# The last product in three fp32r passes instead of two column halves, and one expert tile moved ahead of the second token turn

## The chip, the cores and the metric

The kernel runs on one core of one Trainium2 chip. The metric is the device time of one execution in microseconds (us). The engines that matter are TensorE (PE in the profile: matrix products and transposes), VectorE (DVE), ScalarE (ACT), GpSimd (POOL) and SyncE (SP, whose queue issues the loads). They run side by side and wait for each other on semaphores.

## What is computed

A perceiver block over B = 2 batches of 128 tokens of width 512, with 2048 context rows for each batch, 16 heads, and a feed-forward layer with 4 experts of width 2048. All data is float32. Cut to what matters:

```python
x = x + cross_attention(layernorm(x), ctx, ctx)            # 16 heads, 2048 keys
x = x + self_attention_block(layernorm(x))                 # 16 heads, own residual and layernorm

def ffn(x):                                                # x: (256, 512), called on layernorm(x)
    expert_idx = argmax(x @ W_router)                      # 4 experts
    h = gelu(einsum('th,ehi->tei', x, W1) + b1)            # W1: (4, 512, 2048)
    intermediate = einsum('te,tei->ti', onehot(expert_idx), h)
    y = intermediate @ Wo + bo + x                         # Wo: (2048, 512)
    return layernorm(y) * gamma + beta
x = x + ffn(layernorm(x))
```

## The kernel before

All engines run programs written out by hand, in the order of the code; there is no scheduler. Where one engine needs another's result it waits for a semaphore's count, and everything behind that wait on its engine stands too.

**Two ways to multiply.** A product of float32 operands can be given to TensorE as it is ("whole"). Or each operand is split: a rounded high part H (type fp32r) and the rest L = x - H, and three products HH, HL and LH are added up in PSUM ("three passes"). The large products of the kernel are of the second kind. ACT, POOL or DVE makes H by a copy with a cast, DVE makes L by a subtraction.

**Stages.** The keys, values, scores and the softmax of the cross-attention for batch 0 and then batch 1 take up to about 360 us, eight head groups p after each other, four context chunks c in each (`keys`, `values`, `scores`, `probs_T`, `weighted_values`). In the first group, p = 0, the values V of a chunk are made by four products j = 0 to 3 between `keys(0, c)` and `scores(0, c)`. ACT copies V for j = 0 and 2, DVE for j = 1 and 3. The self-attention of batch 0 lies inside the batch-1 work.

**The expert layer.** W1 comes as 16 tiles of 128 x 2048, first for batch 0 (`first_experts(n)`, tile FIRST[n]) and then again for batch 1 (`second_experts(n)`, tile n). Since the tokens of batch 0 are ready first, PE runs batch 0's tiles between the steps of batch 1's self-attention. Tiles 0, 1, 2, 3 and 14 (WHOLE) are multiplied whole, line 1409, the rest in three passes, lines 1419 to 1421. The H of a tile is line 631 on ACT (line 404 on POOL), its L is line 979 on DVE (`first_low`).

**The token turn.** After tile 12 (n = 12) PE does `normalized_T(1)` (four transposes of the normalized tokens, line 1141, which wait for DVE's `normalize`, line 710), `expert_bias(0)` (line 1446), `logits(1)` (line 1147 with 4 output columns), then tile 13, `masks(1)` and `onehots_T(1)` (lines 1393 and 1401), tile 14 and tile 15. DVE meanwhile does `first_low(13)`, `logits(1)` (line 908), `router(1)`, the token's low part, `first_low(15)`, `onehots_T(1)`, the masked tokens (`masked_both(0)`, line 931) and then the L part of each tile of the second round, line 1121.

**The second round.** `second_experts(n)` are lines 1460 to 1462: 12 passes of 512 columns for each tile. ACT makes w2H (line 644) when a buffer of three is free, DVE makes w2L (line 1121). Between these tiles PE transposes batch 0's hidden units (`hidden_T(0, c)`) and multiplies them by Wo, four quarters of the 2048 hidden units, `ffn_out(0, c)`, line 1478, 4 whole products each.

**The end.** After the last tile PE does `ffn_out(0, 3)`, then `hidden_T(1, c)` for c = 0 to 3 (line 1141), then batch 1's product with Wo in two column halves, line 1604: 16 whole products of 256 columns for columns 0 to 255, and 16 for the others. ACT (line 557) and DVE (line 944) copy the transposed hidden units to SBUF in turn. `finish(b)` on DVE adds the residual, computes mean and variance, and scales. In batch 1 it takes each half as it comes, lines 955 and 956. One step in it is POOL's power for the inverse root, line 378.

## Time and profile before

| | |
|---|---|
| time, median of 3 runs | 516.69 us (516.57 to 518.53) |
| the profiled execution's own time | 517.64 us |
| its span in the trace | 515.9 us |
| granted TensorE clock, mean | 0.995 |
| PE busy | 498.3 us, 97% of the span |
| DVE busy | 299.4 us, 58% |
| ACT busy | 259.8 us, 50% |
| chain that ended last | PE 79%, ACT 9%, DVE 7%, issue 4%, POOL 1% |

Read the table as the frame: the span is what the trace covers, and 1.7 us of the profiled execution's time lie outside it. PE is busy nearly all the time, and 79% of the chain that ended last is PE's own work, so what counts is which instructions PE has to run and where it stands still. A matmul's row shows its latency, not the time that it keeps the engine; the time between the starts of two matmuls is the rate.

### The profile page before, as it was taken

The page shows a single profiled execution, that of the slowest core. Times are in us where ns is not written, and L with a number is a line of the kernel's source. Part 1 is how long each engine was busy: PE and PEld are TensorE (multiplying, and loading weights), DVE is VectorE, ACT ScalarE, POOL GpSimd, SP SyncE. Part 2 cuts the span into 40 slices and gives each one's busy share as a digit, 9 for nine tenths or more (in the row PEclk, how much of TensorE's full clock was granted, in tenths as well). Part 3 has the DMA queues.
Part 4 walks back from the last instruction along what each step waited for, and adds up shares of the span by engine and source line. Part 5 has one row for each costly group of instructions (what it writes and reads, how often), then busy time and mean ns, then how long its engine had stood idle before and what let it go on. Part 6 is the DMA issues. An engine that isn't in the chain of part 4 may idle for free.

```text
span 515.9 us, 9281 instructions
## 1 busy us (share of the span) xinstructions
PE 498.3 (97%) x3762; PEld 383.1 (74%) x3762; DVE 299.4 (58%) x583; ACT 259.8 (50%) x396; POOL 42.2 (8%) x34
## 2 busy tenths in 40 slices
PE   8999999999999999999999999999999999999995
PEld 6886776777777777887877778757695777877664
DVE  4647523546455542436286474588479988965532
ACT  4130119494858641238267649476255735754310
POOL 0220000000298000000000000000002010000000
PEclk9999999999999999999999999999999989999999
DMA  8800000000440022220300000495586998874000
GB/s 290 344 0 1 1 1 0 3 0 3 151 168 11 1 83 83 81 83 1 142 3 2 0 3 1 147 422 249 180 327 248 361 402 302 334 292 164 1 20 20
DMA packets 11497, 63.52 MB, mean 123 GB/s; under 512 B 1600, under 2 KB 2112, under 8 KB 4544
## 3 DMA queue, kind: packets, MB, share of 16 engines
q1 hardware_dynamic: 11168, 62.67, 32.1%
q8 instruction: 30, 0.49, 0.4%
q10 hardware_dynamic: 288, 0.27, 0.2%
q14 instruction: 11, 0.09, 0.1%
HBM read 62.41 MB, written 0.52 MB: 122 GB/s over the span
## 4 chain that ended last, share of the span: by engine, by line
PE 79%; ACT 9%; DVE 7%; issue 4%; POOL 1%; POOLq 0%; ACTq 0%; DVEq 0%
PE ps L1147 35%; PE ps L1217 11%; PE ps L1231 6%; PE ps L1201 5%; ACT Pm L447 4%; PE ps L1460 3%; PE ps L1462 3%; PE ps L1461 3%; PE ps L1478 3%; PE ps L1604 2%; PE ps L1409 1%; ACT PT L455 1%; PE ps L1141 1%; PE ps L1243 1%; DVE w1L L979 1%
## 5 line engine op out<-in xcount | busy, mean ns | idle before, releaser
L455 ACT COPY PT<-ps 128x512 f32<-128x512 f32 x128 | 68.5, 592 | 28.9 <-PE ps L1217 28.9
L745 DVE TENSOR_SCALAR_CACHE_REDUCE Pm<-ps,small 128x512 f32<-128x512 f32 x96 | 66.4, 748 | 28.5 <-PE ps L1201 28.4
L1217 PE MATMUL ps<-ident,Pm 128*128 128x128 f32 x512 | 69.3, 277 | 2.9 <-ACT Pm L447 2.9
L1217 PEld LDWEIGHTS ps<-ident,Pm 128*128 128x128 f32 x512 | 56.5, 141 | 17.7 <-issue 11.0
L447 ACT ACTIVATE Pm<-Pm,small 128x2048 f32<-128x2048 f32 x32 | 64.3, 2011 | 7.4 <-DVE Pm L745 7.3
L725 DVE SCALAR_TENSOR_TENSOR KrL<-ps,small,KrH 128x512 fp32r<-128x512 f32 x32 | 23.9, 747 | 59.2 <-ACT KrH L433 59.2
L1147 PE MATMUL ps<-ctxH,wkH 128*128 128x512 f32 x124 | 51.3, 414 | 0.0
L1147 PE MATMUL ps<-wvH,ctxH 128*128 128x512 f32 x124 | 50.1, 404 | 1.0 <-DVE V L734 1.0
L1147 PE MATMUL ps<-ctxL,wkH 128*128 128x512 f32 x124 | 48.6, 392 | 0.0
L1147 PE MATMUL ps<-ctxH,wkL 128*128 128x512 f32 x124 | 48.5, 391 | 0.0
L1147 PE MATMUL ps<-wvH,ctxL 128*128 128x512 f32 x124 | 48.4, 390 | 0.0
L1147 PE MATMUL ps<-wvL,ctxH 128*128 128x512 f32 x124 | 48.3, 390 | 0.0
L433 ACT ACTIVATE KrH<-ps,small 128x512 fp32r<-128x512 f32 x32 | 22.0, 688 | 44.4 <-PE ps L1147 43.7
L1121 DVE TENSOR_TENSOR w2L<-w2raw,w2H 128x2048 fp32r<-128x2048 f32 x16 | 36.4, 2289 | 11.8 <-ACT w2H L644 11.8
L644 ACT CAST w2H<-w2raw 128x2048 fp32r<-128x2048 f32 x16 | 30.6, 1911 | 19.0 <-PE ps L1462 15.0
L1231 PE MATMUL ps<-PT,V 128*32 128x128 f32 x1024 | 34.6, 276 | 1.0 <-ACT PT L455 1.0
L378 POOL TENSOR_TENSOR small<-small 128x1 f32<-128x1 f32 x10 | 6.8, 678 | 332.3 <-DVE small L706 332.3
L442 ACT COPY V<-ps 128x512 f32<-128x512 f32 x16 | 9.4, 585 | 46.6 <-PE ps L1147 43.9
L1231 PEld LDWEIGHTS ps<-PT,V 128*32 128x32 f32 x1024 | 26.0, 109 | 8.2 <-issue 6.0
L1147 PEld LDWEIGHTS ps<-ctxH,wkH 128*128 128x128 f32 x124 | 23.5, 190 | 10.0 <-issue 5.7
L734 DVE COPY V<-ps 128x512 f32<-128x512 f32 x16 | 11.0, 689 | 33.1 <-PE ps L1147 33.0
L1147 PEld LDWEIGHTS ps<-wvH,ctxH 128*128 128x128 f32 x124 | 23.3, 188 | 7.4 <-DVE V L734 1.4
(219 smaller groups left out, 859.8 us busy)
## 6 DMA issues: line engine op xcount, KB each, us to landing
w1raw<-in_W SPq DMA_DIRECT2D x16, 1024.0 KB, 6.1
w2raw<-in_W SPq DMA_DIRECT2D x16, 1024.0 KB, 5.5
raw<-in_ctxT SPq DMA_DIRECT2D x7, 1024.0 KB, 5.0
woF<-in_ffn_Wo SPq DMA_DIRECT2D x4, 1024.0 KB, 9.2
wo<-in_wo SPq DMA_DIRECT2D x2, 1024.0 KB, 4.8
ctx_first<-in_ctxT SPq DMA_DIRECT2D x4, 256.0 KB, 5.0
wv_raw<-in_xWv SPq DMA_DIRECT2D x2, 512.0 KB, 7.4
wq<-in_xWq SPq DMA_DIRECT2D x1, 1024.0 KB, 12.2
```

The source lines that it names most:

```text
L433: act.activation(KrH[:, c % KR, :], ps[:, bank, :], ACT.Identity, bias=bias3[:, 1, p % G:p % G + 1], scale=1.0).then_inc(k_hi, 1)
L447: act.activation(Pm[:, i, :], Pm[:, i, :], ACT.Exp, bias=mx[:, p % 2, i, C - 1:C], scale=-1.0, accum_out=den[:, p, i:i + 1]).then_inc(exp_ ...
L455: act.copy(PT[:, c % 2, i, :, :].rearrange("p k t -> p (k t)"), ps[:, t_bank(p, c, i), :]).then_inc(pt_done, 1)
L644: act.copy(w2H[n % 3][:], w2raw[n % RING2][:]).then_inc(w1_hi, 1)
L725: dve.scalar_tensor_tensor(KrL[:, c % KR, :], ps[:, bank, :], bias3[:, 1, p % G:p % G + 1], KrH[:, c % KR, :].bitcast(F32), ALU.add, ALU.s ...
L745: dve.tensor_scalar(Pm[:, i, c * CH:(c + 1) * CH], ps[:, i, :], -1.0, mx[:, p % 2, i, c - 1:c] if c else NOT_YET, ALU.mult, ALU.min, accum ...
L1121: dve.tensor_tensor(w2L[n % RING2][:], w2raw[n % RING2][:], w2H[n % 3][:].bitcast(F32), ALU.subtract).then_inc(w1_split, 1)
L1147: mm = pe.matmul(dst, l, r, start=(n == 0), stop=(n == len(pairs) - 1))
L1201: last = pe.matmul(ps[:, i, :], l[q, g, b * T:(b + 1) * T], r[q, c % KR, :], start=(k == 0), stop=(k == len(terms) - 1))
L1217: last = pe.transpose(ps[:, t_bank(p, c, i), j * P:(j + 1) * P], Pm[:, i, c * CH + j * P:c * CH + (j + 1) * P], ident[:])
L1231: last = pe.matmul(ps[q, PV_BANK, 0:T], V[:, c * JT + j, (HPG * g + i) * DH:(HPG * g + i + 1) * DH], PT[:, c % 2, i, j, :], start=(c == 0 ...
L1460: pe.matmul(dst, zH[:, n, :], wH[:, cc], start=(n == 0), stop=False)
```

## The change

Two larger edits and two small ones.

1. **Batch 1's product with Wo.** The column halves are gone. The hidden units of quarter 3 are multiplied whole (4 products of 512 columns), those of quarters 0 to 2 (12 products) in three passes each. For this ACT makes woH (three casts of 128 x 2048, line 691 of the new kernel) after its last w2H and before batch 1's gelu, and DVE makes woL in place of woF (three subtractions, line 1132) after its last w2L. PE transposes quarter 3 first. ACT copies all four quarters (line 696), three of them as the high part hidTH, and DVE makes hidTL (line 1138) before `finish(0)`. `finish(1)` is now the same as `finish(0)`, on all 512 columns after the last pass. `ffn_out` raises f_mm after every quarter, so that DVE knows when it may overwrite woF.
2. **Tile 14 ahead of the turn.** FIRST has 14 before 13, and three tiles (11, 12, 14) instead of two stand between `attention2_out(1)` and the turn. Its load is issued before `second_in(1)` instead of behind it.
3. **Scores of the last chunk in group 0.** `scores(0, 3)` stands behind the first V product of chunk 3 and not behind the fourth. DVE reads those scores before it copies V for j = 1 and 3.
4. Some pairs of semaphores (one for each batch) become one semaphore that counts on; the waits are for the same events.

```diff
-        FIRST = (0, 1, 4, 5, 6, 2, 3, 7, 8, 9, 10, 11, 12, 13, 14, 15)
+        FIRST = (0, 1, 4, 5, 6, 2, 3, 7, 8, 9, 10, 11, 12, 14, 13, 15)
...
             first_in_(13)
-            second_in(1)
             sp.wait_ge(first_tile, USED[9])
             first_in_(14)
+            second_in(1)
...
+            act.wait_ge(woF_in, 16 * KT)
+            for c in range(SPLIT_WO):
+                act.wait_ge(w1_tile, 11 + c)
+                act.copy(woH[c][:], woF[:, KT * c:KT * (c + 1), :]).then_inc(wo_hi, 1)
             gelu(1, range(IC))
-            hidden_T(1, 0)
-            hidden_T(1, 2)
+            for k, c in enumerate((3, 0, 1, 2)):
+                act.wait_ge(hT_mm[1], k + 1)
+                dst = hidTW if c == 3 else hidTH[:, KT * c:KT * (c + 1), :]
+                act.copy(dst[:].rearrange("p k t -> p (k t)") if c == 3 else dst.rearrange("p k t -> p (k t)"),
+                         ps[:, 4 + c, :]).then_inc(hT_act[1], 1)
...
+            for c in range(SPLIT_WO):
+                k = slice(KT * c, KT * (c + 1))
+                dve.wait_ge(wo_hi, c + 1)
+                dve.wait_ge(f_mm, c + 1)
+                dve.tensor_tensor(woL[:, k, :], woF[:, k, :], woH[c][:].bitcast(F32), ALU.subtract).then_inc(wo_split, 1)
             ffn_residual(0)
             ffn_residual(1)
+            for c in range(SPLIT_WO):
+                k = slice(KT * c, KT * (c + 1))
+                dve.wait_ge(hT_act[1], c + 2)
+                dve.tensor_tensor(hidTL[:, k, :], split4(ps[:, 4 + c, :]), hidTH[:, k, :].bitcast(F32), ALU.subtract)\
+                   .then_inc(hT_dve[1], 1)
             finish(0)
-            hidden_T(1, 1)
-            hidden_T(1, 3)
             finish(1)
...
                 for j in range(JT):
                     values(0, c, j)
-                scores(0, c)
+                    if c == C - 1 and j == 0:
+                        scores(0, c)
+                if c < C - 1:
+                    scores(0, c)
...
-            for c in range(KT):
+            for c in (3, 0, 1, 2):
                 hidden_T(1, c)
-            for h in range(2):
-                cols_h = slice(h * CH // 2, (h + 1) * CH // 2)
-                for k in range(IT):
-                    if h == 0 and k % KT == 0:
-                        c = k // KT
-                        pe.wait_ge(hT_dve[1] if c % 2 else hT_act[1], c // 2 + 1)
-                    last = pe.matmul(ps[:, 1 + h, 0:CH // 2], hidT[1][:, k, :], woF[:, k, cols_h], start=(k == 0),
-                                     stop=(k == IT - 1))
-                last.then_inc(f_mm, 1)
+            pe.wait_ge(hT_act[1], 1)
+            pe.wait_ge(hT_dve[0], 1)
+            for k in range(KT):
+                pe.matmul(ps[:, 1, :], hidTW[:, k, :], woF[:, 3 * KT + k, :], start=(k == 0), stop=False)
+            for c in range(SPLIT_WO):
+                pe.wait_ge(wo_split, c + 1)
+                pe.wait_ge(hT_dve[1], c + 1)
+                for k in range(KT):
+                    hH, hL = hidTH[:, KT * c + k, :], hidTL[:, KT * c + k, :]
+                    pe.matmul(ps[:, 1, :], hH, woH[c][:, k, :], start=False, stop=False)
+                    pe.matmul(ps[:, 1, :], hH, woL[:, KT * c + k, :], start=False, stop=False)
+                    last = pe.matmul(ps[:, 1, :], hL, woH[c][:, k, :], start=False,
+                                     stop=(c == SPLIT_WO - 1 and k == KT - 1))
+            last.then_inc(f_mm, 1)
```

How this changes the order in which instructions stand on an engine is shown at the two places that matter.

PE around the token turn, before: `w1H_D` is tile 12, `attnT` the tokens that are turned, `small,qT` the logits, `w1H_A` tile 13, `w1raw_136` tile 14, `w1H_B` tile 15.

```order
L1421 MATMUL ps<-w1H_D,z0L 128x512
L1141 MATMUL ps<-ident,attnT 128x128 x4
L1446 MATMUL ps<-b1H,ohT_121 128x512 x4
L1446 MATMUL ps<-b1L,ohT_121 128x512 x4
L1147 MATMUL ps<-small,qT 128x4 x4
L1419 MATMUL ps<-w1H_A,z0H 128x512
...
L1393 MATMUL ps<-ident,oh_124 128x128 x4
L1401 MATMUL ps<-ident,oh_124 128x128
L1409 MATMUL ps<-w1raw_136,z_129 128x512 x4
L1419 MATMUL ps<-w1H_B,z0H 128x512
```

The same place in the changed kernel, whose lines are numbered anew.

```order
L1432 MATMUL ps<-w1H_D,z0L 128x512
L1420 MATMUL ps<-w1raw_136,z_129 128x512 x4
L1149 MATMUL ps<-ident,attnT 128x128 x4
L1457 MATMUL ps<-b1H,ohT_121 128x512 x4
L1457 MATMUL ps<-b1L,ohT_121 128x512 x4
L1155 MATMUL ps<-small,qT 128x4 x4
L1430 MATMUL ps<-w1H_A,z0H 128x512
...
L1404 MATMUL ps<-ident,oh_124 128x128 x4
L1412 MATMUL ps<-ident,oh_124 128x128
L1430 MATMUL ps<-w1H_B,z0H 128x512
```

Tile 14 went from behind the one-hot transposes to ahead of the token transposes, and tile 15 now follows the one-hot transposes directly.

DVE from the last tile of the second round to the end, before.

```order
L1121 TENSOR_TENSOR w2L_160<-w2raw_154,w2H_163 128x2048
L938 TENSOR_TENSOR attnT<-attnT,rowsF 128x4x128
...
L939 TENSOR_TENSOR x_sb<-x_sb,rowsF 128x512
L961 TENSOR_TENSOR u_119<-ps,attnT 128x512
...
L965 SCALAR_TENSOR_TENSOR u_119<-u_119,small,x_sb 128x512
L944 COPY hidT_172<-ps 128x512 x2
L955 TENSOR_TENSOR uo_173<-ps,attnT 128x256
L956 BN_STATS small<-uo_173 128x6
L955 TENSOR_TENSOR uo_173<-ps,attnT 128x256
L956 BN_STATS small<-uo_173 128x6
```

And in the changed kernel.

```order
L1121 TENSOR_TENSOR w2L_160<-w2raw_154,w2H_163 128x2048
L1132 TENSOR_TENSOR woL<-woF,woH_174 128x2048
L1132 TENSOR_TENSOR woL<-woF,woH_175 128x2048
L1132 TENSOR_TENSOR woL<-woF,woH_176 128x2048
L948 TENSOR_TENSOR attnT<-attnT,rowsF 128x4x128
...
L949 TENSOR_TENSOR x_sb<-x_sb,rowsF 128x512
L1138 TENSOR_TENSOR hidTL<-ps,hidTH 128x512 x3
L961 TENSOR_TENSOR u_119<-ps,attnT 128x512
...
L961 TENSOR_TENSOR uo_173<-ps,attnT 128x512
L712 BN_STATS small<-uo_173 128x6
```

Six subtractions are new on DVE: three large ones ahead of the residuals and three small ones ahead of `finish(0)`, where two copies had stood behind it. The half-width additions and statistics became full-width ones.

## Rows read from the trace of the kernel before

**Rows 1.** Timeline, PE at the end: start us, us, engine, line, operation, [idle before].
```profile
489.63 3.59 PE L1478 MATMUL ps<-woF,hidT 128*128 128x512 f32 x8
...
493.06 1.91 PE L1141 MATMUL ps<-ident,hid 128*128 128x128 f32 x16
...
494.80 1.89 PE L1604 MATMUL ps<-woF,hidT 128*128 128x256 f32 x8
...
497.73 12.35 PE L1604 MATMUL ps<-woF,hidT 128*128 128x256 f32 x56 [1.03 <-DVE hidT L944]
```
**Rows 2.** The same timeline, first and last pass of one second-round tile's stretch.
```profile
486.90 0.39 PE L1460 MATMUL ps<-w2H,zH 128*128 128x512 f32 x1
...
489.40 0.39 PE L1462 MATMUL ps<-w2H,zL 128*128 128x512 f32 x1
```
**Rows 3.** The same timeline, DVE: `finish(0)`'s first and last step, then `finish(1)`'s.
```profile
493.33 0.69 DVE L961 TENSOR_TENSOR u<-ps,attnT 128x512 f32<-128x512 f32 x1 [8.95 <-PE ps L1478]
...
496.32 0.75 DVE L965 SCALAR_TENSOR_TENSOR u<-u,small,x_sb 128x512 f32<-128x512 f32 x1 [0.51 <-POOL small L378]
...
510.19 0.42 DVE L955 TENSOR_TENSOR uo<-ps,attnT 128x256 f32<-128x256 f32 x1 [6.09 <-PE ps L1604]
...
512.68 0.75 DVE L965 SCALAR_TENSOR_TENSOR uo<-uo,small,x_sb 128x512 f32<-128x512 f32 x1 [0.51 <-POOL small L378]
```
**Rows 4.** The same timeline, ACT and DVE ahead of the end.
```profile
477.37 1.90 ACT L644 CAST w2H<-w2raw 128x2048 fp32r<-128x2048 f32 x1 [0.80 <-PE ps L1462]
...
479.30 2.29 DVE L1121 TENSOR_TENSOR w2L<-w2raw,w2H 128x2048 fp32r<-128x2048 f32 x1 [0.41 <-ACT w2H L644]
...
487.78 2.64 ACT L552 ACTIVATE hid<-ps 128x512 f32<-128x512 f32 x4 [8.51 <-PE ps L1462]
...
493.69 0.59 ACT L557 COPY hidT<-ps 128x512 f32<-128x512 f32 x1 [3.27 <-PE ps L1141]
```
**Rows 5.** Timeline, PE around the token turn.
```profile
418.32 0.39 PE L1421 MATMUL ps<-w1H_D,z0L 128*128 128x512 f32 x1
419.59 0.66 PE L1141 MATMUL ps<-ident,attnT 128*128 128x128 f32 x4 [0.87 <-DVE attnT L710]
...
421.01 1.10 PE L1147 MATMUL ps<-small,qT 128*128 128x4 f32 x8
421.97 0.78 PE L1419 MATMUL ps<-w1H_A,z0H 128*128 128x512 f32 x1
...
426.33 0.60 PE L1393 MATMUL ps<-ident,oh 128*128 128x128 f32 x4
...
433.08 0.39 PE L1460 MATMUL ps<-w2H,zH 128*128 128x512 f32 x1
```
**Rows 6.** Stretches: us, busy of PE, PEld, DVE, ACT, POOL, then granted clock, DMA.
```profile
422.00:425.00 3.00, 3.00 (x8) 2.42 (x9) 2.62 (x8) 2.95 (x2) 0.00 (x0) 0.50 0.99 418
```
**Rows 7.** Timeline, DVE behind the turn.
```profile
422.14 0.16 DVE L908 COPY small<-ps 128x4 f32<-128x4 f32 x1 [0.41 <-PE ps L1147]
...
424.00 2.28 DVE L979 TENSOR_TENSOR w1L<-w1raw,w1H_B 128x2048 fp32r<-128x2048 f32 x1
427.08 0.29 DVE L927 CAST ohT<-ps 128x128 fp32r<-128x128 f32 x1 [0.80 <-PE ps L1401]
...
428.80 4.49 DVE L1121 TENSOR_TENSOR w2L<-w2raw,w2H 128x2048 fp32r<-128x2048 f32 x2
```
**Rows 8.** Timeline, SyncE's queue: the load of tile 14.
```profile
407.14 0.33 SPq L298 DMA_DIRECT2D w1raw<-in_W  x1
```
**Rows 9.** The page's DMA issues: KB each, median us from issue to landing.
```profile
w1raw<-in_W SPq DMA_DIRECT2D x16, 1024.0 KB, 6.1
```
**Rows 10.** Timeline, PE and ACT between group 0 and group 1.
```profile
76.87 2.01 ACT L447 ACTIVATE Pm<-Pm,small 128x2048 f32<-128x2048 f32 x1 [3.82 <-DVE Pm L745]
...
78.62 0.39 PE L1147 MATMUL ps<-ctxL,wkH 128*128 128x512 f32 x1
...
79.05 0.69 ACT L433 ACTIVATE KrH<-ps,small 128x512 fp32r<-128x512 f32 x1
```

More of the change, by code:

```diff
@@ L152, in perceiver_block @@
         uo = [u[0], at("uo_1", [P, D], F32, 182)]
+        SPLIT_WO = 3
+        woH = [at(f"woH{c}", [P, KT, D], F32R, kb) for c, kb in enumerate((64, 80, 128))]
+        woL = at("woL", [P, SPLIT_WO * KT, D], F32R, 96)
+        hidTH = at("hidTH", [P, SPLIT_WO * KT, T], F32R, 56)
+        hidTW = at("hidTW", [P, KT, T], F32, 62)
+        hidTL = at("hidTL", [P, SPLIT_WO * KT, T], F32R, 184)
         col = [0]
@@ L247, in perceiver_block @@
             sem("v2T_mm"), sem("v2_ready"), sem("pv2_mm"), sem("rden_ready"), sem("cN_ready"))
-        cT_dve, cT_act, o2_mm, u_done = each("cT_dve"), each("cT_act"), sem("o2_mm"), sem("u_done")
+        cT_dve, cT_act, o2_mm, u_done = sem("cT_dve"), sem("cT_act"), sem("o2_mm"), sem("u_done")
         x2T_mm, x2T_done, logit_mm, logit_done, z_ready = (
@@ L504, in features @@
                     act.activation(dst[b][:, m, :], ps[:, QKV_BANKS[b][k], m * T:(m + 1) * T], ACT.Identity,
-                                   bias=b2[:, k, m:m + 1], scale=1.0).then_inc(ready[b], 1)
-                act.wait_ge(ready[b], KT)
+                                   bias=b2[:, k, m:m + 1], scale=1.0).then_inc(ready, 1)
+                act.wait_ge(ready, KT * (b + 1))
             def exponentials2(b, i):
@@ L800, in _ @@
                     split(c + 1)
-                for j in (1, 3):
-                    values(0, c, j)
+                if c < C - 1:
+                    values(0, c, 1)
+                    values(0, c, 3)
                 if c == 1:
@@ L1475, in ffn_out @@
                 pe.wait_ge(woF_in, 16 * KT)
+                if c == 0 and b:
+                    pe.wait_ge(hT_dve[0], 1)
                 pe.wait_ge(hT_dve[b] if c % 2 else hT_act[b], c // 2 + 1)
@@ L1575, in _ @@
             attention2_out(1)
-            for n in range(11, 13):
+            for n in range(11, 14):
                 first_experts(n)
@@ L1595, in _ @@
             ffn_out(0, 3)
-            for c in range(KT):
+            for c in (3, 0, 1, 2):
                 hidden_T(1, c)
-            for h in range(2):
-                cols_h = slice(h * CH // 2, (h + 1) * CH // 2)
-                for k in range(IT):
-                    if h == 0 and k % KT == 0:
-                        c = k // KT
-                        pe.wait_ge(hT_dve[1] if c % 2 else hT_act[1], c // 2 + 1)
-                    last = pe.matmul(ps[:, 1 + h, 0:CH // 2], hidT[1][:, k, :], woF[:, k, cols_h], start=(k == 0),
-                                     stop=(k == IT - 1))
-                last.then_inc(f_mm, 1)
+            pe.wait_ge(hT_act[1], 1)
+            pe.wait_ge(hT_dve[0], 1)
+            for k in range(KT):
[9 more added lines that the diff above has]
+                                     stop=(c == SPLIT_WO - 1 and k == KT - 1))
+            last.then_inc(f_mm, 1)
 ROWS = ("L0_xattn_bo", "L0_attn_bo", "L0_attn_beta", "L0_attn_gamma",
```

54 lines of the change are left out of this document (21 added, 33 removed).

## The prediction

> **What bounds the kernel now.** I read the page first: PE is busy for 97% of the span and carries 79% of the chain that ended last, so only PE's instructions and its halts count. Then the timeline of the last 26 us, since most of the diff is there. PE never stops from the last expert tile to the transposes; then come 8 half-width matmuls, a halt for DVE's copy of the hidden units, and 56 more [rows 1]. Behind PE's last matmul there is only `finish(1)`, on DVE and POOL [rows 3]. Then the token turn: PE halts for 0.87 us for the normalized tokens, does small work up to 421.97 [rows 5], and the granted clock of the next three microseconds is 0.50, that is 1.2 GHz instead of 2.4 [rows 6]. Last the border of groups 0 and 1 [rows 10].
>
> **The rates.** A whole product of 512 columns is two matmul records; four take from 489.63 to 493.06, 3.43 us, or 0.857 each [rows 1]. A half-width matmul takes 12.35 / 56 = 0.2205 us, so a half product takes 0.441 and the 32 of them 64 x 0.2205 = 14.1 us [rows 1]. An fp32r pass of 512 columns takes (489.40 - 486.90) / 11 = 0.2273 us [rows 2], so three passes take 0.682, less than the whole product's 0.857.
>
> The Trainium skill ("TensorE: Matmul & The Clock Gate", Back-to-back issue gap) gives columns / 2.4 GHz plus 2.5 ns for a lone matmul's gap, 216 ns here. The measured 227 ns is what I use; by the page's figure the new end would be 0.4 us shorter still, by an estimate.
>
> **Edit 1, the end.** Both kernels reach the first product with Wo at about 494.7: `ffn_out(0, 3)` ends at 493.06 and the 16 transposes take 1.64 us [rows 1]. Before, from there to PE's end at 510.08: 14.1 us of matmuls and a gap of 497.73 - 494.70 - 8 x 0.2205 = 1.27 us behind the DVE copy [rows 1]; 15.4 together. Now: 4 whole products, 3.43, and 36 passes, 36 x 0.2273 = 8.18; 11.6 together, if nothing waits. PE is done at 506.3, 3.8 us earlier.
>
> Does anything wait? Each new operand in turn. woH: ACT's last w2H ends at 479.27 [rows 4]. The buffers that woH overwrites belong to tiles 10, 11 and 12, which are done by then (the last cast itself waited for tile 12), so three casts of 1.90 end at 485.0. Gelu begins at 487.78 [rows 4]: 2.8 us of slack, and the casts cost nothing. woL: DVE is free at 481.6, three subtractions of 2.29 end at 488.5 [rows 4], and the two residual pairs, four full-width steps of 0.69 [rows 3] and their waits, 2.9 us, at 491.4. hidT: the first transposes are quarter 3's, which needs the last gelu. That ends at 487.78 + 2.64 = 490.4, covered until 493.06 by `ffn_out(0, 3)`. ACT's copy starts at 493.69 and lasts 0.59 [rows 4], so it ends at 494.28, before 494.7. Then three more copies, about 0.5 us apart, end near 495.8, and DVE's three hidTL of about 0.69 near 496.8. The first pass needs the first of them at 494.7 + 3.43 = 498.1. So this wait has 2.5 us of slack. The DVE halt vanishes, and no other takes its place. `finish(0)` is moved behind hidTL and runs from about 496.8 to 500.6; its store is long over at the end.
>
> The end behind PE gets longer. `finish(1)` was half-width, from 510.19 to 513.43, 3.24 us. Now it is full-width, as `finish(0)` is: 493.33 to 497.07, 3.74 us [rows 3]. So 0.5 us are lost there, and I allow 0.1 for the wider last matmul. Sum of edit 1: 3.8 - 0.5 - 0.1 = **3.2 us** gained. Bounds: 2.2 us (one more halt of about 1.0, like the one of rows 1) and 3.6.
>
> **Edit 2, tile 14 ahead.** It is multiplied whole, 3.43 us, from 418.55 to 421.98. Its load is issued at 407.14 and no longer behind that of a second-round tile [rows 8]; 11.4 us remain until its use, against a median of 6.1 for the loads of such tiles [rows 9], so I charge no wait. It covers the 0.87 us halt, since that halt ends at 419.59 [rows 5]. The turn then goes from 421.98: transposes 0.43, bias and ACT's copy, logits from 423.3 to 424.3, which is 2.3 us later than the 421.97 of before [rows 5]. Between full matmuls PE has now 2.3 us of light work, where it had 3.4, so I expect the clock to stay at 2.4 GHz. In the trace the half clock cost 426.33 - 421.97 - 2.82 = 1.5 us in tile 13 (12 passes of 0.2273 and a restart of 0.1 are 2.82) [rows 5].
>
> But behind the turn DVE now decides. Its chain starts with the logits' copy, and from there to the start of `first_low(15)` are 1.86 us, then 2.28 [rows 7]. The copy moves from 422.14 to 424.46, so tile 15's low part is ready at 428.6, and PE, through with tile 13 at 427.1 and with the one-hot transposes at 427.7, waits **0.9 to 1.0 us**; before, tile 14 stood there. Tile 15 runs to 431.5. DVE goes on: the one-hot copy 0.3, the two masked products 1.2, w2L of tile 0 2.2 [rows 7], done at 432.4. **Another 0.9 us.** The second round starts at 432.4 instead of 433.08 [rows 5]. Then w2L(1), masked_both(1) and w2L(2), 2.2 + 1.2 + 2.3, end at 437.9 or 438.0, and PE's third tile would start then; before, it started at 433.08 + 2 x 2.72 = 438.5. From there on PE is the bound. So edit 2 gains **0.5 us** against this trace. Bounds: if the clock falls all the same in tile 13, its 1.5 us mostly fill the waits, and w2L(2) comes at about 438.8: a loss of 0.4. If both waits were absent, the gain would be 0.87 + 1.5 = 2.4.
>
> Against an execution of before whose clock did not fall, the same arithmetic goes the other way: there PE would reach the third tile at 436.9, and the 438.0 of the changed kernel is 1.1 us worse. That execution would take about 517.64 - 1.6 = 516.0; the two shorter runs, 516.57 and the median 516.69, lie 0.5 above this, the profiled one 1.0 above them.
>
> The Trainium skill ("TensorE: Matmul & The Clock Gate", What's actually happening) says that the gate's window is free-running and not tied to the kernel's start, so that the same program can meet it differently from run to run. One trace can't show that; it would make the fall at 422 a property of some executions of before.
>
> **Edit 3, scores of the last chunk.** They come 8.2 us earlier (three V products of 12 passes). ACT's first exponential, at 76.87 [rows 10], can start at about 74.0, behind its V copy. But the next thing on ACT is the high part of `keys(1, 0)` at 79.05, and that needs PE's product, whose last matmul starts at 78.62 in either order [rows 10]; the other three exponentials follow it. So 2.8 us on ACT turn into waiting: **0**. Bounds 0.2 either way, the restart that PE saves at its own next wait there. **Edit 4** counts the same events: 0.
>
> **Sum.** 517.64 - 3.2 - 0.5 - 0 = 513.9 against the profiled execution. The end of the changed kernel doesn't depend on which execution of before it is set against; since the ordinary runs lie somewhat above what I work out for them, I say **514.0 us**, 2.7 less than the median, or 0.52%.
>
> **Rivals.**
> - *The turn costs nothing* (DVE is quicker, or the waits shorter than I think): up to 1.9 more, 512.1. Against it: the DVE rows behind the logits are back to back. Chance 0.08.
> - *The clock falls once more* around the two new waits, or in tile 13: the turn's gain goes, and up to 1.6 us. 514.8 to 515.5. For it: there are now three light spots (422 to 424.3, 427.1 to 428.7, 431.5 to 432.4) instead of one. Against it: each is shorter than the one that had the fall. Chance 0.15.
> - *One operand of the passes is late*: hidTL waits behind ACT's copies, DVE runs woL later than I think, and a halt of about 1 us opens at 498. 515.0. Against it: 2.5 us of slack. Chance 0.07.
> - *Slower than before*: the clock falls and stays down over more than one stretch, since the spots follow each other. Each stretch like the one at 422 costs PE about 1.6 us. From two on, with the end as forecast, 513.9 + 3.2 = 517.1, above the median; from four on it would be over 0.5% slower. Chance 0.04.
> - *Tile 14 ahead gains nothing, as the wait only moves*, is half of my forecast already: with the clock left out of the count, it does lose.
>
> **How the numbers follow.** The forecast, 513.6 to 514.6, has 0.66. 0.5% of 516.69 is 2.6 us, about what a measurement of this kernel can tell from no change; the border, 514.1, cuts through it. A bit over half of it and the first rival lie below: faster 0.49. The rest of it, the late operand, the single clock fall and most of the fourth are within: 0.48. Slower 0.03. The range from 512.9 to 515.4 leaves out most of the first rival and all of the fourth.
>
> **What would show it.** Right: 36 passes at 0.227 us with no halt at their start, PE's last matmul 3.8 us nearer to the transposes, 3.74 us from there to the last DVE step; a halt of 0.9 us ahead of tile 15 for line 979's successor and one of 0.9 ahead of the first second-round tile for w2L; clock 1.00 throughout. Wrong: a halt between the whole products and the first pass, gelu starting later than the last tile allows, a granted clock under 1.00 after 422, or the high part of `keys(1, 0)` earlier than 79.05.

## The result and the profile after

| | before | changed kernel |
|---|---|---|
| median, 12 runs each | 518.48 us (516.57 to 520.54) | 515.26 us (514.85 to 516.63) |
| the profiled execution's own time | 517.64 us | 515.1 us |
| its span | 515.9 us | 513.3 us |
| granted TensorE clock, mean | 0.995 | 0.998 |

The ratio is 0.9945 (of the means; of the medians it is 0.9938), with a 95% interval of 0.993 to 0.9961: faster by 0.55%. The forecast was 514.0 us, 512.9 to 515.4. The measured median is 1.3 us above the 514.0 and only 0.14 us inside the top of the range. The ratio taken on 518.48 gives 515.6, with an interval of 514.9 to 516.5, for the most part above the range. As a ratio the forecast was 514.0 / 516.69 = 0.9948: the gain came out as said, the level did not. How much of that agreement is luck is told under "The base" below.

The page's totals and PE's waits come first (engine, line, waited for: us in total, times, longest).

```profile
PE 495.2 (96%) x3742; PEld 378.2 (74%) x3742; DVE 307.7 (60%) x585; ACT 266.2 (52%) x401; POOL 42.2 (8%) x34
...
PE ps L1430 <- DVE w1L L979: 0.8, 1, 0.8
...
PE ps L1471 <- DVE w2L L1121: 0.6, 1, 0.6
PE ps L1149 <- DVE attnT L718: 0.5, 1, 0.5
```

PE has 3 us less work. The halt of 0.87 for the tokens and the one of 1.03 for the hidden units [rows 1, 5] are gone, and two new ones stand ahead of tile 15 (0.8) and of the second round (0.6), the two places that the prediction named.

The timeline at the end, PE (start us, us, engine, line, operation), answers to [rows 1]. 33 rows of the same spacing are left out behind L1619.

```profile
493.51 1.91 PE L1149 MATMUL ps<-ident,hid 128*128 128x128 f32 x16
495.25 3.60 PE L1612 MATMUL ps<-woF,hidTW 128*128 128x512 f32 x8
498.29 0.79 PE L1618 MATMUL ps<-woH,hidTH 128*128 128x512 f32 x1
498.92 0.39 PE L1619 MATMUL ps<-woL,hidTH 128*128 128x512 f32 x1
...
506.67 0.39 PE L1620 MATMUL ps<-woH,hidTL 128*128 128x512 f32 x1
```

No row there has an [idle before], the note of a halt. From 495.25 to 498.92, less one pass, are 3.44 us for the four whole products; the last 34 intervals take (506.67 - 498.92) / 34 = 0.228 us each. The forecast had 3.43 and 0.2273.

The timeline of the operands of those passes, ACT and then DVE, and the last DVE steps; it answers to [rows 3, 4].

```profile
479.62 5.52 ACT L691 CAST woH<-woF 128x2048 fp32r<-128x2048 f32 x3
488.24 2.64 ACT L557 ACTIVATE hid<-ps 128x512 f32<-128x512 f32 x4 [3.10 <-PE ps L1473]
494.15 0.59 ACT L696 COPY hidTW<-ps 128x512 f32<-128x512 f32 x1 [3.27 <-PE ps L1149]
494.63 1.57 ACT L696 CAST hidTH<-ps 128x512 fp32r<-128x512 f32 x3
```
```profile
481.96 6.69 DVE L1132 TENSOR_TENSOR woL<-woF,woH 128x2048 fp32r<-128x2048 f32 x3
...
495.32 1.89 DVE L1138 TENSOR_TENSOR hidTL<-ps,hidTH 128x512 fp32r<-128x512 f32 x3 [3.90 <-ACT hidTH L696]
...
507.10 0.69 DVE L961 TENSOR_TENSOR uo<-ps,attnT 128x512 f32<-128x512 f32 x1 [6.24 <-PE ps L1620]
...
510.09 0.75 DVE L965 SCALAR_TENSOR_TENSOR uo<-uo,small,x_sb 128x512 f32<-128x512 f32 x1 [0.51 <-POOL small L383]
```

The three casts end at 485.14, ahead of gelu by 3.1 us. The three woL end at 488.65. The first hidTL is ready near 496.0, and PE wants it at 498.3: 2.3 us of slack, forecast 2.5. From 507.10 to 510.84 are 3.74 us, as forecast.

The token turn on PE answers to [rows 5]: tile 14 is L1420, the tokens L1149, the logits L1155, tile 13 begins at 425.21, tile 15 at 429.57, the second round at 433.27.

```profile
419.52 3.59 PE L1420 MATMUL ps<-w1raw,z 128*128 128x512 f32 x8
422.95 0.60 PE L1149 MATMUL ps<-ident,attnT 128*128 128x128 f32 x4
...
424.32 1.03 PE L1155 MATMUL ps<-small,qT 128*128 128x4 f32 x8
425.21 0.48 PE L1430 MATMUL ps<-w1H_A,z0H 128*128 128x512 f32 x1
...
428.49 0.27 PE L1412 MATMUL ps<-ident,oh 128*128 128x128 f32 x1
429.57 0.50 PE L1430 MATMUL ps<-w1H_B,z0H 128*128 128x512 f32 x1 [0.81 <-DVE w1L L979]
...
433.27 0.47 PE L1471 MATMUL ps<-w2H,zH 128*128 128x512 f32 x1 [0.64 <-DVE w2L L1121]
```

The stretch of tile 13, which had half the clock before [rows 6] (same columns: length, busy of PE, PEld, DVE, ACT, POOL, granted clock, DMA):

```profile
425.00:428.40 3.40, 3.40 (x20) 2.83 (x20) 2.77 (x8) 3.28 (x2) 0.00 (x0) 1.00 1.01 426
```

### The profile page after: what moved, and what is told of

It is laid out like the page before. It is cut to its first block, busy times and chain, and to the rows that moved or that the text cites. A ratio compares the mean times of both kernels' runs of the same rounds, so it can differ in the third digit from the quotient of the medians.

```text
span 513.3 us, 9255 instructions
## 1 busy us (share of the span) xinstructions
PE 495.2 (96%) x3742; PEld 378.2 (74%) x3742; DVE 307.7 (60%) x585; ACT 266.2 (52%) x401; POOL 42.2 (8%) x34
## 4 chain that ended last, share of the span: by engine, by line
PE 83%; ACT 7%; DVE 5%; issue 4%; POOL 0%; POOLq 0%; ACTq 0%; DVEq 0%
PE ps L1155 36%; PE ps L1225 11%; PE ps L1239 6%; PE ps L1209 5%; ACT Pm L452 4%; PE ps L1471 3%; PE ps L1473 3%; PE ps L1472 3%; PE ps L1491 3%; PE ps L1430 1%; PE ps L1431 1%; PE ps L1432 1%; PE ps L1149 1%; PE ps L1420 1%; ACT PT L460 1%
## 5 line engine op out<-in xcount | busy, mean ns | idle before, releaser
L1155 PE MATMUL ps<-wvH,ctxH 128*128 128x512 f32 x124 | 50.3, 405 | 1.0 <-DVE V L742 1.0
L1155 PE MATMUL ps<-ctxH,wkH 128*128 128x512 f32 x124 | 51.1, 412 | 0.0
L1155 PE MATMUL ps<-ctxL,wkH 128*128 128x512 f32 x124 | 48.6, 392 | 0.0
L1155 PE MATMUL ps<-ctxH,wkL 128*128 128x512 f32 x124 | 48.5, 391 | 0.0
L1155 PE MATMUL ps<-wvH,ctxL 128*128 128x512 f32 x124 | 48.4, 390 | 0.0
L1155 PE MATMUL ps<-wvL,ctxH 128*128 128x512 f32 x124 | 48.3, 390 | 0.0
L1155 PEld LDWEIGHTS ps<-ctxH,wkH 128*128 128x128 f32 x124 | 23.5, 190 | 9.3 <-issue 5.0
L1155 PEld LDWEIGHTS ps<-wvH,ctxH 128*128 128x128 f32 x124 | 23.3, 188 | 8.0 <-issue 2.0
```

What stands on the lines that cost most here:

```text
L1155: mm = pe.matmul(dst, l, r, start=(n == 0), stop=(n == len(pairs) - 1))
```

## The experiments

The theory at the start was the prediction's: the end gains 3.2 us whatever the clock does; tile 14 ahead removes a fall of the clock (1.5 us) and buys it with two halts for DVE; edit 3 is worth nothing. The rivals: the end gains less, the tile nothing, or the fall has nothing to do with the turn. No experiment leaves a part of the computation out; three add products whose results nobody reads, as is said there.

### The end without the tile, the tile without the end, the scores alone

e1_wo is the changed kernel with FIRST, its loads and the order of tiles put back (edits 1, 3 and 4 left). e2_tile is the kernel before with edit 2. e3_scores is the kernel before with edit 3.

```diff
 e1_wo (against the changed kernel)
-        FIRST = (0, 1, 4, 5, 6, 2, 3, 7, 8, 9, 10, 11, 12, 14, 13, 15)
+        FIRST = (0, 1, 4, 5, 6, 2, 3, 7, 8, 9, 10, 11, 12, 13, 14, 15)
...
 e3_scores (against the kernel before)
                 for j in range(JT):
                     values(0, c, j)
-                scores(0, c)
+                    if c == C - 1 and j == 0:
+                        scores(0, c)
+                if c < C - 1:
+                    scores(0, c)
```

> Edits 1, 3 and 4 without edit 2: the tile order and the turn are as before. My theory (the end gives 3.2 us, edit 3 nothing): 2.9 to 3.4 us faster than the kernel before, ratio about 0.9938, and in the profile 36 passes at 0.227 us right behind the four whole products. The rival that the gain of the pair comes from the turn: the ratio would be over 0.998. The rival that one operand is late: a halt of 1 us at the first pass, 2.2 us faster.

> Edit 2 alone on the kernel before. My theory: against an execution in which the clock fell in tile 13 it gains 0.5 us, against one in which it stayed up it loses 1.1 us; the profile has a halt of about 0.8 us ahead of tile 15 (line 979's w1L) and of about 0.6 to 0.9 ahead of the first second-round tile. Since single runs of before lie 4 us apart (516.6 to 520.5), more than one fall of the clock (1.6 us) explains, the median should be between 0.5 lower and 1.1 higher. The rival that edit 2 also keeps the clock up, and that this is worth more than the waits: 1 to 2 us faster, and a much smaller spread of its runs than that of before.

> Edit 3 alone on the kernel before. My theory: no change, within 0.2 us; in the profile the first exponential starts at about 74 instead of 77 us, and the high part of the next group's keys where it did, 0.43 us behind the start of PE's last matmul. The rival that the earlier scores shorten the border of the groups: 0.5 us or more, and a shorter halt of PE for the fourth exponential.

| | runs | median us | ratio to before | 95% |
|---|---|---|---|---|
| e1_wo | 10 | 515.84 | 0.9948 | 0.9926 to 0.997 |
| e2_tile | 12 | 518.17 | 0.9994 | 0.9977 to 1.0012 |
| e3_scores | 12 | 517.8 | 0.9999 | 0.9978 to 1.002 |

All of the gain that the medians can tell is the end's; edits 2 and 3 alone can't be told from nothing. e1_wo was expected at 0.9938, which its interval holds; the rival for e2_tile, that the tile keeps the clock up and makes it 1 to 2 us faster, fails by the medians. But the single runs fall into groups by their mean granted clock, and there the tile does something. Over the 67 runs of the kernel before that lay beside the experiments:

| mean granted clock | runs | median us | from, to |
|---|---|---|---|
| 0.997 and more | 27 | 517.14 | 516.18, 517.85 |
| 0.995 and 0.996 | 30 | 518.56 | 518.08, 519.62 |
| 0.993 and less | 10 | 520.22 | 519.78, 520.64 |

The steps are 1.4 and 1.7 us, near the 1.5 us that the fall at 422 had cost [rows 5, 6]. The groups don't overlap in time. That the two upper steps are one fall and two falls is read from their size: the profiled execution of the kernel before has the middle group's clock and one fall, and none of the lowest group was profiled. e1_wo has two runs at 0.998 (513.99, 514.11), seven at 0.994 and 0.995 (515.09 to 516.72) and one at 0.991 (517.14): the same ladder, 2.7 to 3.1 us lower. e2_tile has no such ladder: all 12 at 0.997 to 1.0, from 517.28 to 518.58. So the tile does remove the fall, and it does cost about 1 us against a run without one (518.17 - 517.14), as the prediction had it (1.1).

The mean clock alone can't be carried from kernel to kernel. It covers the whole span, and behind PE's last matmul it reads 0.50 once more, where that costs nothing. This last stretch begins near 514.0 us in the kernel before, 511.1 in the changed one, 511.0 in e7_whole and 508.6 in e6_finish_first. The last two were profiled at a mean of 0.996 without a fall anywhere else. Two stretches of e7_whole, the turn and the end, where no matmul is left (x0):

```profile
421.00:426.00 5.00, 4.65 (x31) 3.63 (x32) 4.42 (x10) 4.06 (x4) 0.00 (x0) 1.00 1.00 424
511.00:514.00 3.00, 0.00 (x0) 0.00 (x0) 1.04 (x2) 0.00 (x0) 0.69 (x1) 0.50 0.19 72
```

So 0.996 tells of a fall only together with the time; no profiled execution without one has a mean below 0.996. What does not depend on it is the length of the same piece of work in the traces, from `wo,cT` to batch 1's last transposes: 81.79 us in both executions that had the old turn and no fall (e3_scores, e7_whole), 83.39 in both that had one (before, e1_wo), 82.90 and 82.87 with the tile (e2_tile, the changed kernel). A fall costs 1.60 us there, and the tile 1.1 us more than no fall.

The halts of e2_tile are those of the changed kernel, 0.81 us for w1L and 0.68 for w2L:

```profile
429.93 0.50 PE L1419 MATMUL ps<-w1H_B,z0H 128*128 128x512 f32 x1 [0.81 <-DVE w1L L979]
...
433.62 0.47 PE L1460 MATMUL ps<-w2H,zH 128*128 128x512 f32 x1 [0.68 <-DVE w2L L1121]
```

e3_scores gave a view that was not expected: its profiled execution has the same turn as before, the halt included, and the clock did not fall in it. The stretch 422 to 425, e3_scores, then e1_wo, where it did (0.57):

```profile
422.00:425.00 3.00, 3.00 (x18) 2.59 (x18) 2.42 (x9) 3.00 (x3) 0.00 (x0) 1.00 1.02 429
```
```profile
422.00:425.00 3.00, 3.00 (x11) 2.45 (x11) 2.41 (x9) 3.00 (x2) 0.00 (x0) 0.57 1.01 421
```

The instructions are the same, and at the full clock 18 records of them begin in these three microseconds, at the lower one 11. So the fall is a property of the execution, not of the program alone. e7_whole, which also keeps the old turn and its halt of 0.87 us, shows the same. The Trainium skill ("TensorE: Matmul & The Clock Gate", What's actually happening) says that the gate's window is free-running. These runs fit that, with 27 of 67 executions of one program at the top of the ladder and 40 below it; no run here sets where the window stands, so that it is the reason is not shown.

### Is it the light work in the turn?

e5_fill puts eight products of the identity with itself (results unused) behind tile 12 and ahead of the tokens' transposes, in the kernel before; e10_wo_fill does so in e1_wo. e11_light goes the other way: in the kernel before, eight tiny ones of 4 columns behind the logits.

```diff
+            pe.wait_ge(u_done, 2)
+            for n in range(8):
+                pe.matmul(ps[:, PV_BANK, 0:P], ident[:], ident[:], start=True, stop=True)
             normalized_T(1)
             expert_bias(0)
```
```diff
             logits(1)
+            for n in range(8):
+                pe.matmul(ps[:, PV_BANK, 0:E], ident[:], ident[:, 0:E], start=True, stop=True)
             first_experts(13)
```

> The kernel before with 8 small matmuls on the identity (their result is not used) in the halt ahead of the second token turn. Of 33 runs of before, those at a mean clock of 0.997 and more took 516.6 to 517.9 us and those at 0.996 and less 518.1 to 520.6. My theory, that light work around the turn lets the clock fall in some executions: all runs at 0.997 or more, median 516.9 to 517.2 us, the longer times gone, 1 to 1.5 us below the median of before. The rival that the clock falls elsewhere, or that filling 0.87 of 3.4 light us is too little: the same mix of 517 and 518 to 520 us as before.

> Edits 1, 3 and 4 without edit 2 and with the same 8 small matmuls. In the runs of this pair without the fill, those at 0.998 took 514.0 us and those at 0.995 515.1 to 516.7. My theory: median near 514.0 us with a narrow spread, that is 1.2 us better than the changed kernel, whose halts behind the turn cost this. The rival: as without the fill, 514 to 517 us, median 515.8.

> The kernel before with 8 more tiny matmuls (4 columns, result not used) behind the logits of the turn, so that the light stretch there is about 1 us longer, 4.4 instead of 3.4. It turns the fill upside down. My theory, that the light stretch decides whether the clock falls: nearly all runs at 0.996 or less, median 519 to 519.5 us, few or none at 517 to 518. The rival that the falls have to do with something else: the mix of before shifted by at most 1 us, 518 to 521 with a third of the runs still at 0.998.

e5_fill: 517.48 us (516.99 to 518.16, 11 runs), ratio 0.9974 (0.9961 to 0.9987). No run is below a clock of 0.996 or above 518.16 us, while 12 of the 14 runs of the kernel before beside it took 518.1 us or more, at clocks of 0.996 and less. e10_wo_fill: 514.19 us (513.99 to 515.49, 5 runs), ratio 0.9925 (0.9907 to 0.9944). The turn of e5_fill:

```profile
419.61 1.95 PE L1580 MATMUL ps<-ident 128*128 128x128 f32 x16
421.39 0.60 PE L1141 MATMUL ps<-ident,attnT 128*128 128x128 f32 x4
```

The eight products take 1.78 us, 0.9 more than the halt that they fill, and the kernel is faster all the same. This is the clean test: neither the order nor the loads nor DVE's work was touched, and the ladder went away. The overshoot is seen in the traces: from `wo,cT` to the last transposes e5_fill takes 82.50 us and e10_wo_fill 82.46, 0.7 more than the 81.79 without a fall. By medians e5_fill stays 0.3 us above the top group of the kernel before, and above the 516.9 to 517.2 that was expected of it. What it shows is that the fall needs the halt or the light stretch at its full length; whether products of 4 columns without a halt would do it was not tried.

e11_light: 521.76 us over six runs, of which the profiled one took 999.3 us and is left out of what follows; the others are 520.3, 521.41, 521.58, 521.93 and 524.08 at clocks of 0.990 to 0.995, ratio 1.0073 (1.0045 to 1.0102). Every one of them lost clock. Eight more tiny products cost 3.8 us by the ratio, where 519 to 519.5 us had been expected. The direction is what the theory wants; the size is above every number that was set down for it. There is no usable profile of it, so where the clock was lost, and how often, is open.

### Can the two new halts be had away?

e4_split15 pulls the split of tile 15 ahead of the turn, on ACT and on DVE, in the changed kernel. e8_load15 adds an earlier load. e9_low0 adds w2L of the first second-round tile ahead of the one-hot copy and the masks.

```diff
 e4_split15: ACT, then DVE
+            first_high(15, 11)
             transposed(yT[1], x2T_mm, 1, XT_BANKS[1], x2T_done)
             transposed(yTH, x2T_mm, 1, XT_BANKS[1], yT_hi)
-            first_high(15, 11)
...
             first_low(13)
+            dve.wait_ge(first_hi_act, 6)
+            first_low(15)
             logits(1)
 e8_load15: SyncE, besides
+            sp.wait_ge(first_tile, USED[10])
+            first_in_(15)
             second_in(1)
 e9_low0: DVE, besides
+            second_low(0)
             onehots_T(1)
             dve.wait_ge(mask_done, 2)
```

> The changed kernel, with tile 15's high part (ACT) ahead of the turned tokens' copies and its low part (DVE) ahead of the logits. ACT stands idle for 9.7 us and DVE for 2.7 us just there. My theory, that DVE's chain behind the logits makes the two new halts: both halts vanish, the second round starts 1.5 to 2 us earlier, 1.4 to 1.9 us faster than the changed kernel, ratio to before about 0.991. The rival that tile 15's load lands too late (11.8 us after its issue at 410.8, so at 422.6): the cast starts at 422.6, delays the tokens' copy by about 1 us and the gain is 0.5 us or less.

> The changed kernel with tile 15's split ahead of the turn, as in the run where its cast waited for the load until 422.64 us, and with the load of tile 15 issued ahead of second_in(1) and of the three broadcast rows. My theory: the load lands about 4 us earlier, near 418.5; the cast no longer holds up the tokens' copy, no halt ahead of tile 15. What is left is the halt ahead of the second round, since the one-hot copy, two masks and w2L of its first tile take 4.1 us against tile 15's 2.7: 1.4 us. So about 1 us earlier than the changed kernel at the second round, median near 514.3 us. The rival that the reordered loads make another tile late: a new halt for w1raw or w2raw, no gain.

> The kernel before last, and w2L of the second round's first tile made by DVE ahead of the one-hot copy and the masks, which it doesn't need. My theory: no halt from tile 14 to the second round's third tile but the one inside the turn; the second round starts 1.9 us earlier than in the changed kernel, median 513.2 to 513.5 us, ratio to before 0.991. The rival that the masks, now later by 2.2 us, are what PE waits for: then the halt ahead of the second round stays at 1 us or more and the time is that of the kernel before it.

| | runs | median us | ratio to before | 95% |
|---|---|---|---|---|
| e4_split15 | 12 | 516.57 | 0.9972 | 0.9953 to 0.9991 |
| e8_load15 | 5 | 514.3 | 0.9924 | 0.9907 to 0.9941 |
| e9_low0 | 4 | 513.62 | 0.991 | 0.9892 to 0.9928 |

e4_split15 was slower than the changed kernel. Its ACT says why, and e8_load15's edit answers it. ACT in e4_split15, then in e9_low0:

```profile
422.64 1.90 ACT L636 CAST w1H_B<-w1raw 128x2048 fp32r<-128x2048 f32 x1 [8.56 <-DMA w1raw<-in_W]
424.44 0.58 ACT L494 COPY qT<-ps 128x512 f32<-128x512 f32 x1
```
```profile
417.48 1.91 ACT L636 CAST w1H_B<-w1raw 128x2048 fp32r<-128x2048 f32 x1 [3.08 <-PE ps L1438]
424.06 0.59 ACT L494 COPY qT<-ps 128x512 f32<-128x512 f32 x1 [4.68 <-PE ps L1155]
```

In e4_split15 tile 15 was not there: its load is issued at 411.00, behind that of a second-round tile and three of rows, and takes 11.6 us to land (11.8 in the changed kernel, where the two loads of such tiles ahead of it took 6.2 and 6.4). The tokens' copy then stood behind the cast on ACT, and PE halted 0.77 us for it ahead of the logits, in the light stretch itself; 8 of 12 runs had a clock of 0.993 or less. And the halt ahead of tile 15 had only moved: the one ahead of the second round was 1.44 us, where the changed kernel had 0.64, since DVE still made the masked products before w2L. With the load ahead of that tile the copy is no longer held up, and the 1.44 us stay, as was expected (e8_load15). e9_low0, which has that load too, makes w2L first: the cast runs at 417.48 and ACT then idles 4.68 us. The turn of e9_low0 on PE, L1436 tile 15, L1477 the second round:

```profile
428.53 0.60 PE L1410 MATMUL ps<-ident,oh 128*128 128x128 f32 x4
428.96 0.27 PE L1418 MATMUL ps<-ident,oh 128*128 128x128 f32 x1
428.99 0.48 PE L1436 MATMUL ps<-w1H_B,z0H 128*128 128x512 f32 x1
...
431.84 0.40 PE L1477 MATMUL ps<-w2H,zH 128*128 128x512 f32 x1
```

Neither halt is left. The second round starts at 431.84, where the changed kernel had 433.27; counted from `wo,cT` (411.11 and 410.64) it is 1.90 us earlier, as expected. e9_low0 is the fastest of all versions and beats both kernels: 4.9 us below the kernel before in its own comparison (518.56), and its interval, 0.9892 to 0.9928, lies below the changed kernel's, 0.993 to 0.9961, though it rests on four runs. Its gain has three parts that the runs tell apart: no fall, no cost for having none, and the end.

### The end taken apart

e7_whole is the kernel before with its last product undivided: 16 whole products of 512 columns, and `finish(1)` full-width. e6_finish_first is the changed kernel with `finish(0)` ahead of hidTL.

```diff
 e7_whole
-            for h in range(2):
-                cols_h = slice(h * CH // 2, (h + 1) * CH // 2)
...
+            for k in range(IT):
+                last = pe.matmul(ps[:, 1, :], hidT[1][:, k, :], woF[:, k, :], start=(k == 0), stop=(k == IT - 1))
...
 e6_finish_first
+            finish(0)
             for c in range(SPLIT_WO):
...
-            finish(0)
             finish(1)
```

> The kernel before with batch 1's last product in 16 whole products of 512 columns, without halves and without fp32r passes. By the terms of the prediction: 32 matmuls of 0.4285 us, 13.7, instead of 14.1; the halt of 1.27 us for DVE's copy is covered, since the first quarter now takes 3.43 us; the work behind PE is 0.6 us longer. Sum: 1.1 us faster than before, and what the twelve products in passes add is 12 x (0.857 - 0.682) = 2.1 us. The rival that the halves were worth their price because of the shorter work behind PE: 0.5 us slower. The halt in the halves of before is what decides.

> The changed kernel with finish(0) ahead of the three hidTL on DVE. It tests the slack of hidTL: finish(0) takes 3.74 us from about 494.1 to 497.8, so the first hidTL ends at 498.5 and the first pass, which now starts at about 498.7, waits for less than 0.1 us. My theory: the time of the changed kernel, within 0.2 us, and no halt of over 0.2 us at line 1618. The rival that hidTL stands on the critical path: up to 3 us slower.

e7_whole: 516.55 us (12 runs) beside 517.37 of the kernel before, 0.8 us less by medians; ratio 0.9977 (0.9959 to 0.9996), which is 1.2 us. 1.1 were expected. PE and the last DVE steps:

```profile
494.87 13.90 PE L1592 MATMUL ps<-woF,hidT 128*128 128x512 f32 x32
```
```profile
508.80 0.69 DVE L951 TENSOR_TENSOR uo<-ps,attnT 128x512 f32<-128x512 f32 x1 [10.47 <-PE ps L1592]
```

Its last DVE step ends at 512.54, 19.42 us behind the transposes at 493.12. The kernel before had 20.37 from the same point, the changed kernel 17.33. So 0.95 us of edit 1's 3.04 are not the passes at all, and 2.09 are. The column halves had let PE run into the halt of 1.03 us after 8 matmuls of 0.22 us [rows 1]; four whole products of 0.857 cover the same copies. The 2.09 are twelve products at 0.682 and not at 0.857, 2.1 us.

e6_finish_first: 515.0 us median over six runs (a seventh took 707 us and is left out); ratio 0.9953 (0.9928 to 0.9979), no difference from the changed kernel. hidTL starts 3.94 us behind the transposes at 493.10, where it was 1.81 in the changed kernel, and PE still does not stop:

```profile
497.04 1.88 DVE L1139 TENSOR_TENSOR hidTL<-ps,hidTH 128x512 fp32r<-128x512 f32 x3
...
497.88 0.79 PE L1618 MATMUL ps<-woH,hidTH 128*128 128x512 f32 x1
```

The slack of 2.3 us is real: 2.1 of it were taken here at no cost. The place of `finish(0)` doesn't matter.

## Why the prediction was right, and where it was wrong

Here is the same account on the two profiled executions, in the order of the program, from rows of both.

| stretch | before | after | difference | forecast |
|---|---|---|---|---|
| start to the first transposes of `xn` | 21.68 | 22.40 | +0.72 | 0 |
| from there to `wo,cT` (edits 3 and 4 lie in it) | 387.99 | 388.24 | +0.25 | 0 |
| from there to the third second-round tile (edit 2) | 28.85 | 28.24 | -0.61 | -0.5 |
| from there to the last transposes | 54.54 | 54.63 | +0.09 | 0 |
| from there to the last DVE step's end (edit 1) | 20.37 | 17.33 | -3.04 | -3.2 |

The rows that part the stretches, before and then after:

```profile
21.68 1.04 PE L1141 MATMUL ps<-ident,xn 128*128 128x128 f32 x8
...
409.67 1.88 PE L1147 MATMUL ps<-wo,cT 128*128 128x512 f32 x4
...
438.52 0.39 PE L1460 MATMUL ps<-w2H,zH 128*128 128x512 f32 x1
```
```profile
22.40 0.93 PE L1149 MATMUL ps<-ident,xn 128*128 128x128 f32 x7
...
410.64 1.02 PE L1155 MATMUL ps<-wo,cT 128*128 128x512 f32 x2
...
438.88 0.47 PE L1471 MATMUL ps<-w2H,zH 128*128 128x512 f32 x1
```

**The step that failed: the first term of "517.64 - 3.2 - 0.5 - 0 = 513.9 against the profiled execution", taken as the level of the kernel before.** The differences were right within 0.2 us each; the execution that they were taken from was a lucky one. Among the 12 profiled executions that can be used (both kernels and ten experiments) the transposes of `xn` start from 21.68 to 23.02, with a middle near 22.4; the kernel before shown at first had the earliest. The edits don't order them: e1_wo, with three of the four, has 21.96, e2_tile 22.44, e5_fill 22.67 and e7_whole, which has none, 23.02. So 0.72 of the 1.1 us that separate the two sums is the draw of the start. The next 0.25 is of the same kind: e3_scores, with edit 3 alone, has 387.80 for that stretch, e1_wo, with edits 3 and 4, 388.17, and e7_whole, with neither, 388.31.

The start has two draws in it. The kernel opens with 28 matmul records on the identity, and the products with `ctx_first` follow them. The opening, before, then e3_scores:

```profile
1.54 5.22 PE L1243 MATMUL ps<-ident 128*128 128x128 f32 x28 [1.54 <-POOL ident L372]
```
```profile
1.55 6.21 PE L1246 MATMUL ps<-ident 128*128 128x128 f32 x28 [1.55 <-POOL ident L372]
```

The trace's record of the granted clock begins, at full speed, at 5.40 us in the first and at 7.48 in the second (ahead of that there is none), and the products with `ctx_first` start at 6.60 and 7.59. In five executions (before, e1_wo, e3_scores, e5_fill, e6_finish_first) the transposes of `xn` come 15.06 to 15.08 us behind that start, the shortest of the twelve, so among these the whole difference is made before the first product on data. The other draw is the loads. ACT's second cast of `wv_raw`, which waits for a load, starts at 10.94 in the kernel before, 11.70 in the changed one and 12.29 in e7_whole, and in these three the transposes come 10.70 to 10.74 behind it. Of the 0.72 us, 0.26 are the start of the products with `ctx_first` (6.60 and 6.86), and the other 0.46 opened behind it, with the late load. What draws the one or the other was not tried.

**The range was too tight with it.** It held the median by 0.14 us, and four of the 12 runs lie above its top, 515.4. The range had the sizes of the edits and of the halts in it, and not the 1.3 us by which executions with the same beginning differ in their start. The prediction did see that two of the three runs shown lay below the profiled one, and that its own arithmetic put a run without the fall at 516.0, below both of them (by 0.57 and 0.69, where it says 0.5); it then added 0.1 to the sum. The 517.14 of 27 runs says that 516.0 was 1.1 too low. The early start makes 0.74 of that against the middle of the 12 (22.42) and the stretch behind it 0.13 (387.99 against 388.12); 0.2 to 0.3 are not accounted for. The same two, 0.87 together, are nearly all by which the profiled execution's 517.64 lies below its own group's 518.56. Had the sum been made against a run of that kind, 517.14 - 3.2 + 1.1 = 515.0 would have come out; 515.26 was measured. The 1.1 is the prediction's own price of the tile against a run without a fall, and the traces have it as 1.1 too (82.9 and 81.79).

**The base.** 516.69 was the median of three runs, two of them without a fall by their times (516.57 and 516.69). Over 12 runs it is 518.48, since of the 67 beside the experiments 40 have one. What the change is worth depends on which of them it is set against: 1.9 us against those at 0.997 and more (517.14 - 515.26), 3.3 against the middle group. That the forecast ratio, 0.9948, and the measured one, 0.9945, agree so closely is therefore luck in part: the first is set against a base mostly without a fall, the second against one mostly with it.

**Edit 1, 3.2 forecast.** 3.04 in the traces, and 3.1 between the top groups (517.14 and 514.05, e1_wo). Nothing waits, as said. Of the 0.16 short, 0.10 are a misreading: the transposes take 1.74 us in both kernels (494.80 - 493.06 in [rows 1]), and the prediction counted 1.64, which also made the gap of before 1.27 and not 1.17. The rest is mostly the last matmul's row, which ends 0.39 behind its start where 0.1 had been allowed for all that is wider.

**Edit 2, 0.5 gained against a fall, 1.1 lost without.** 0.6 in the traces; by medians of groups, e1_wo at 0.994 and 0.995 has 515.85 and the changed kernel 515.26, 0.6 gained, and e1_wo at 0.998 has 514.05, 1.2 lost. Tile 15 and the second round were forecast for 428.6 and 432.4; moved by the 0.97 by which this execution was late at `wo,cT`, that is 429.57 and 433.37, and 429.57 and 433.27 were measured. The halts read 0.81 and 0.64, where 0.9 to 1.0 and 0.9 were said, as the profile counts them from the end of a matmul's latency. Which of the two cases a run gets was left open in the prediction; the runs close it: 40 of 67 fall, by clock and time together.

**Edit 3, 0.** e3_scores at 0.9999 says so. The exponential started at 74.81, where about 74.0 plus the 0.7 of the start was forecast, and ACT then idled for `keys(1, 0)`:

```profile
74.81 2.01 ACT L452 ACTIVATE Pm<-Pm,small 128x2048 f32<-128x2048 f32 x1
...
79.77 0.69 ACT L438 ACTIVATE KrH<-ps,small 128x512 fp32r<-128x512 f32 x1 [2.86 <-PE ps L1155]
```

79.77 is 0.72 behind the 79.05 of before [rows 10]: the start's difference, and nothing else.

**The rivals.** One came in part. "Tile 14 ahead gains nothing, as the wait only moves", which had neither a time nor a chance of its own, is what e2_tile's 0.9994 says of edit 2 over the mix of executions, and the waits did move to where the prediction put them. "The clock falls once more" had 514.8 to 515.5 for its time, and the measured median lies in it, but for another reason: the profiled execution had 1.00 in tile 13, where the fall had been, and 11 of the 12 runs have a mean of 0.996 or more and no time above 515.64. The twelfth, 516.63 at 0.995, looks like a fall; it was not the profiled one.

## What to carry to other kernels

A sum of differences is only as good as the execution that it is added to: look where the shown one stands among its runs (the start, the clock) before you name a time, and let the range hold that spread even if every edit is priced well. In this kernel a short halt next to light work on TensorE cost more than itself, in some executions only. Filling it with idle products cost nothing but their overshoot, and it showed at once that the clock was at stake. When a tile is moved ahead of a turn, the engine that makes its successor's operands, and the load that it is made from, have to move with it.

## What the runs showed of the hardware

- One program, one input: 27 of 67 executions at a mean granted clock of 0.997 or more, 30 at 0.995 or 0.996, 10 at 0.993 or less, with medians of 517.14, 518.56 and 520.22 us. In the two profiled executions with a fall (before, e1_wo) it lies behind a halt of 0.87 us, transposes, biases and 1.1 us of products with 4 columns, where full products then ran at 1.2 GHz and not 2.4 (granted clock 0.50 and 0.57 from 422 to 425 us). It cost 1.60 us (83.39 against 81.79 for the same work).
- Behind PE's last matmul the clock reads 0.50 as well, and this alone takes the mean of the ten profiled executions without a fall to between 0.999 and 0.996. A mean clock is compared within one kernel, and with the time beside it.
- Eight identity products in that halt ended it: 16 runs of two kernels at 0.996 to 1.0. Eight products of 4 columns more made it worse: five of five runs at 0.990 to 0.995, 520.3 to 524.08 us.
- Executions of programs with the same beginning reach the same product at 21.68 to 23.02 us. One part is how long the opening products of the identity take (5.22 to 6.22 us), the other when a load is there (the second cast of `wv_raw` starts at 10.65 to 12.29 us).
- With the DMA engines full, a load of 1 MB took 11.6 and 11.8 us from issue to landing behind others, and 6.2 and 6.4 us in the same stretch ahead of them (DMA share 1.00 from 411 to 417 us in the changed kernel). With its issue moved ahead of them (e8_load15), no load of such a tile took more than 6.4 us.
